# Attention scores of two steps side by side in PSUM, worked on in pairs

## The reference

```
xn  = layernorm(x)
q,k,v = xn @ Wq.T, xn @ Wk.T, xn @ Wv.T          16 heads of 32
s   = softmax(causal(q k^T / sqrt(32))) v         then @ Wo.T
h   = silu(xn @ W1.T) * (xn @ W3.T)               2048 wide
g   = silu(fwht(h) @ W2.T)                        Walsh-Hadamard transform of h
out = x + s * g
```

## Time and profile before

| | |
|---|---|
| runs (3) | median 944.87 us, 943.33 to 947.14 |
| profiled execution | 944.66 us, span 943.0 us |
| granted TensorE clock | 0.999 of full speed |
| busy share of the span | PE 98%, PEld 60%, DVE 77%, ACT 66%, POOL 36% |
| DMA | 110.09 MB, 117 GB/s in the mean |
| `heads` of batch one, of batch two | first score matmul at 88.4 us, at 556.3 us |

### The profile page before, as it was taken

How to read it: one execution, slowest core, us unless ns; L and a number is a source line. 1 busy time by engine, 2 the same in 40 slices (tenths; PEclk the granted TensorE clock), 3 DMA queues, 4 the chain that set the end, 5 groups by cost and what they waited for, 6 DMA issues and landing times. The chain is left out here.

```text
span 943.0 us, 19017 instructions
## 1 busy us (share of the span) xinstructions
PE 928.3 (98%) x6500; PEld 566.6 (60%) x6500; DVE 728.0 (77%) x1416; ACT 625.5 (66%) x1340; POOL 339.0 (36%) x591
## 2 busy tenths in 40 slices
PE   8999999999999999999999999999999999999997
PEld 7764566666666656744468656566665666575443
DVE  7886998998998988846665579989898899833343
ACT  4456889989889877833344358787887888833221
POOL 1896664665665442000000114344344353410000
PEclk9999999999999999999999999999999999999999
DMA  9797245544343414661236622323323232150111
GB/s 291 270 252 228 80 114 151 143 118 118 86 121 90 118 31 124 221 226 44 67 103 244 201 57 80 91 58 95 76 75 92 61 81 58 46 202 22 45 45 45
DMA packets 57920, 110.09 MB, mean 117 GB/s; under 512 B 5600, under 2 KB 22624, under 8 KB 57312
## 3 DMA queue, kind: packets, MB, share of 16 engines
q1 hardware_dynamic: 57824, 108.88, 38.9%
HBM read 79.23 MB, written 29.36 MB: 115 GB/s over the span
## 5 line engine op out<-in xcount | busy, mean ns | idle before, releaser
L1264 DVE TENSOR_TENSOR p_lo<-stages,p_hi 128x512 f16<-128x512 f32 (+2 forms) x288 | 201.7, 710 | 25.3 <-ACT p_hi L878 23.7
L1613 PE MATMUL f<-x_hi,w_lo 128*128 128x512 f16 x512 | 195.6, 382 | 0.0
L1613 PE MATMUL f<-x_lo,w_hi 128*128 128x512 f16 x512 | 194.8, 380 | 0.0
L1613 PE MATMUL f<-x_hi,w_hi 128*128 128x512 f16 x512 | 194.5, 380 | 0.0
L868 ACT ACTIVATE stages<-s 128x512 f32<-128x512 f32 (+2 forms) x288 | 150.6, 524 | 57.9 <-PE s L1573 55.5
L878 ACT ACTIVATE p_hi<-stages 128x512 f16<-128x512 f32 (+2 forms) x288 | 160.5, 557 | 25.6 <-POOL stages L699 16.4
L1573 PE MATMUL s<-qk_st 98*128 98x512 f32 (+2 forms) x384 | 129.9, 416 | 1.7 <-DMA qk_st<-m_lo 1.5
L699 POOL TENSOR_SCALAR_AFFINE_SELECT stages<-stages 128x128 f32<-128x128 f32 x192 | 61.4, 325 | 167.9 <-ACT stages L868 167.4
L707 POOL TENSOR_TENSOR w_lo<-w,w_hi 128x256 f16<-128x256 f32 x128 | 95.5, 775 | 55.2 <-ACT w_hi L931 52.8
L1251 DVE CUSTOM_DVE_ANT_0 m<-m,causal 128x1024 f32<-128x1024 f32 (+1 forms) x98 | 104.5, 1066 | 3.8 <-PE m L1554 2.7
L986 ACT ACTIVATE h_hi<-hidden 128x1024 f16<-128x1024 f32 x32 | 33.8, 1057 | 97.1 <-PE f L1411 97.1
(11 more groups left out here) (224 smaller groups left out, 1907.9 us busy)
## 6 DMA issues: line engine op xcount, KB each, us to landing
qk_st<-qk_parts SPq DMA_DIRECT2D x96, 256.0 KB, 4.3
w<-w1w SPq DMA_DIRECT2D x32, 512.0 KB, 3.6
qk_parts<-qk_hi SPq DMA_DIRECT2D x32, 256.0 KB, 3.5
qk_parts<-qk_lo SPq DMA_DIRECT2D x32, 256.0 KB, 4.4
scan<-w1w SPq DMA_DIRECT2D x12, 512.0 KB, 5.6
wht_in<-w SPq DMA_DIRECT2D x4, 1024.0 KB, 10.6
w_butterflied<-wht_in SPq DMA_DIRECT2D x4, 1024.0 KB, 5.7
x_in<-x SPq DMA_DIRECT2D x16, 256.0 KB, 2.9
```

Of the source, the lines that this page charges most:

```text
L1264: dve.tensor_tensor(p_lo[s][:], expd[q % NE][:, 0:end - need], p_hi[s][:], ALU.subtract).then_inc(p_lo_done, 1)
L1613: mm = pe.matmul(F[m][:, 0, :], w, v, start=k == 0, stop=k == GMM - 1)
```

## The change

Two steps, 2u and 2u + 1, make a pair u (6 in a head, NP). Their scores are written to two adjacent PSUM banks, the odd step's right-aligned in the first and the even step's left-aligned in the second, so that what is kept of both lies in one run of columns: 896, 384, 1024, 1024, 896 and 384 columns for pairs 0 to 5. PE issues the odd step's matmul first and signals once for the pair, and waits for the exponential of the whole pair before. One `exp`, one `probs_hi` and one `probs_lo` work on a pair: `exp` in ACT's slot 2u, `probs_hi` in ACT's slot 2u + 1, `probs_lo` in DVE's slot 2u + 1. One select masks both diagonal tiles of a pair. `expd` becomes two buffers of 1024 columns in room of their own, in place of four of 512 of which three were the `stages`. On SP the loads of w2 for the tail no longer wait for the last `probs_lo`. POOL's w13_low pieces wait for the exponentials of pairs 1 and 2, two pieces each, where they waited for those of steps 3, 4, 5 and 6. The two slab parts on POOL at a head's end come after the last mask and no longer between masks. Other counts in waits are rewritten from steps to pairs, the one of `transpose_ctx` (L1659) too, which is not shown.

```diff
...
 NS = len(STEPS)
+NP = NS // 2
 MAX_ORDER = [7, 0, 5, 1, 6, 2, 4, 3]
-NE = 4
+NE = 2
...
                 xt_lo = sb("xt_lo", [P, KT, S], F32R, q)
-            p_hi = [sb(f"p_hi{s}", [P, widths[s]], F16, r) for s in range(NS)]
-            p_lo = [sb(f"p_lo{s}", [P, widths[s]], F16, r) for s in range(NS)]
+            p_hi = [sb(f"p_hi{u}", [P, widths[2 * u] + widths[2 * u + 1]], F16, r) for u in range(NP)]
+            p_lo = [sb(f"p_lo{u}", [P, widths[2 * u] + widths[2 * u + 1]], F16, r) for u in range(NP)]
             squares = sb("squares", [P, 2 * D], F16, r)
-            sb("room_after_p", [P, 4 * KT * S - 2 * sum(widths) - 2 * D], F16, r)
+            expd = [sb(f"expd{i}", [P, 2 * W], F32, r) for i in range(NE)]
+            sb("room_after_p", [P, 4 * KT * S - 2 * sum(widths) - 2 * D - 4 * NE * W], F16, r)
...
             w13_lo = [w13_lo0, sb("w13_lo1", [P, 2, D], F16, r)]
-            expd = [*stage, sb("expd3", [P, W], F32, r)]
             scan = sb("scan", [P, 2, D], F32, r)
-            sb("room_before_o", [P, 5 * P], F32, r)
+            sb("room_before_o", [P, W + 5 * P], F32, r)
...
         F = [bank("f0"), bank("f1")]
-        SB = [bank("s0"), bank("s1")]
+        S_PAIR = bank("s", 2)
+        SB = [S_PAIR[:, i:i + 1, :] for i in range(2)]
...
-        def masks_before(n, s):
-            return n * NT + sum(diagonal(i) is not None for i in range(s))
+        def masked_pair(u):
+            return diagonal(2 * u) is not None
+        def masks_upto(n, u):
+            return n * (NT // 2) + sum(masked_pair(i) for i in range(u + 1))
+        def pair_widths(u):
+            return widths[2 * u + 1], widths[2 * u]
+        def in_pair(parts, s):
+            w1, w0 = pair_widths(s // 2)
+            return parts[s // 2][:, 0:w1] if s % 2 else parts[s // 2][:, w1:w1 + w0]
+        def pair_bank(u):
+            w1, w0 = pair_widths(u)
+            return S_PAIR[:].rearrange("p b w -> p (b w)")[:, W - w1:W + w0]
         def hidden_part(n, c):
...
                     if j + 2 < NH:
-                        after(sp, scores_ps, n * NS)
+                        after(sp, scores_ps, n * NP)
...
                                  ).then_inc(wo_in, 16)
-                sp.wait_ge(p_lo_done, (n0 + NH) * NS)
...
                     sp.wait_ge(wht_stored, D // P * 16)
+                    sp.wait_ge(w13_sum, SCAN_FIRST)
...
-            def mask(q):
-                pool.wait_ge(exp_done, q + 1)
+            def mask(n, u):
+                pool.wait_ge(exp_done, n * NP + u + 1)
                 pool.sem_inc(mask_begun, 1)
-                e = expd[q % NE][:, 0:P]
-                pool.affine_select(out=e, in_=e, compare_op=ALU.is_ge, fill=0.0, base=0, pattern=[[1, P]],
+                e = expd[(n * NP + u) % NE][:, 0:2 * pair_widths(u)[0]].rearrange("p (a c) -> p a c", a=2)[:, :, 0:P]
+                pool.affine_select(out=e, in_=e, compare_op=ALU.is_ge, fill=0.0, base=0, pattern=[[0, 2], [1, P]],
...
             def w13_low(n, piece):
...
             def heads(b):
...
                     n = b * NH + j
-                    for s in range(TPC):
-                        mask(n * NS + s)
+                    for u in range(TPC // 2):
+                        mask(n, u)
...
                         for piece in range(4):
-                            pool.wait_ge(exp_done, n * NS + 4 + piece)
+                            pool.wait_ge(exp_done, n * NP + 2 + piece // 2)
...
                         late_steps(1)
-                    mask(n * NS + 2 * TPC)
+                    mask(n, TPC)
                     combine(n, 0)
-                    for s in range(2 * TPC + 1, NS):
-                        mask(n * NS + s)
-                        if n < LAST_SLAB_AT - 1 and s >= NS - 2:
+                    mask(n, TPC + 1)
+                    for part in range(2):
+                        if n < LAST_SLAB_AT - 1:
...
                         of = j - LAST_SLAB_AT
-                        if b == 0 and 0 <= of < 8 and s >= NS - 2:
-                            slab_step(D // P - 1, of // 2, of % 2, s - NS + 2)
+                        if b == 0 and 0 <= of < 8:
+                            slab_step(D // P - 1, of // 2, of % 2, part)
...
             def exp(q):
-                c, k = STEPS[q % NS]
-                start, need, end = score_cols(c, k)
+                u = q % NP
...
                 after(act, p_lo_done, q - NE + 1)
-                act.activation(expd[q % NE][:, 0:end - need], SB[q % 2][:, 0, need - start:end - start],
-                               ACT.Exp).then_inc(exp_done, 1)
+                act.activation(expd[q % NE][:, 0:sum(pair_widths(u))], pair_bank(u), ACT.Exp).then_inc(exp_done, 1)
             def probs_hi(q):
-                n, s = divmod(q, NS)
-                _, need, end = score_cols(*STEPS[s])
+                n, u = divmod(q, NP)
                 act.wait_ge(exp_done, q + 1)
-                if diagonal(s) is not None:
-                    act.wait_ge(mask_done, masks_before(n, s) + 1)
-                after(act, pv_done, q - NS + 1)
-                act.activation(p_hi[s][:], expd[q % NE][:, 0:end - need], ACT.Copy
+                if masked_pair(u):
+                    act.wait_ge(mask_done, masks_upto(n, u))
+                after(act, pv_done, (n - 1) * NS + 2 * u + 2)
+                act.activation(p_hi[u][:], expd[q % NE][:, 0:sum(pair_widths(u))], ACT.Copy
...
             def copy_o(n, c):
...
                         copy_o(n0 + j - 1, 1)
-                    if g < SLOTS:
-                        exp(n0 * NS + g)
-                    if 1 <= g <= SLOTS:
-                        probs_hi(n0 * NS + g - 1)
+                    if g < SLOTS and g % 2 == 0:
+                        exp(n0 * NP + g // 2)
+                    if g < SLOTS and g % 2 == 1:
+                        probs_hi(n0 * NP + g // 2)
...
             def probs_lo(q):
-                s = q % NS
-                _, need, end = score_cols(*STEPS[s])
+                u = q % NP
                 dve.wait_ge(p_hi_done, q + 1)
-                dve.tensor_tensor(p_lo[s][:], expd[q % NE][:, 0:end - need], p_hi[s][:], ALU.subtract
+                dve.tensor_tensor(p_lo[u][:], expd[q % NE][:, 0:sum(pair_widths(u))], p_hi[u][:], ALU.subtract
...
             def split_wo(b, kt):
                 if kt == 0:
-                    dve.wait_ge(scores_ps, (b * NH + NH - 1) * NS)
+                    dve.wait_ge(scores_ps, (b * NH + NH - 1) * NP)
...
                         maxima(n0 + jm, r)
-                    if 1 <= g <= SLOTS:
-                        probs_lo(n0 * NS + g - 1)
+                    if g < SLOTS and g % 2 == 1:
+                        probs_lo(n0 * NP + g // 2)
...
             def scores(q):
-                n, s = divmod(q, NS)
-                c, k = STEPS[s]
-                start, _, end = score_cols(c, k)
-                if s == 0:
+                n, u = divmod(q, NP)
+                if u == 0:
                     pe.wait_ge(m_in, (n + 1) * 32)
-                after(pe, exp_done, q - 1)
-                pe.matmul(SB[q % 2][:, 0, 0:end - start], k_st[n % NH % 3][0:STACK + 2, k * P:(k + 1) * P],
-                          q_st[n % NH % 3][0:STACK + 2, start:end], start=True, stop=True).then_inc(scores_ps, 1)
+                after(pe, exp_done, q)
+                for s in (2 * u + 1, 2 * u):
+                    c, k = STEPS[s]
+                    start, _, end = score_cols(c, k)
+                    bank = SB[0][:, 0, W - (end - start):W] if s % 2 else SB[1][:, 0, 0:end - start]
+                    mm = pe.matmul(bank, k_st[n % NH % 3][0:STACK + 2, k * P:(k + 1) * P],
+                                   q_st[n % NH % 3][0:STACK + 2, start:end], start=True, stop=True)
+                mm.then_inc(scores_ps, 1)
             def context(q):
...
                     after(pe, o_copied, n * NC + c)
-                pe.wait_ge(p_lo_done, q + 1)
+                pe.wait_ge(p_lo_done, q // 2 + 1)
...
-                    pe.matmul(O[:, 0, first:first + VN], p_hi[s][:, at:at + P], v, start=k == 0 and t == c * TPC, stop=False,
+                    pe.matmul(O[:, 0, first:first + VN], in_pair(p_hi, s)[:, at:at + P], v, start=k == 0 and t == c * TPC, stop=False,
                               skip_group_check=True)
-                    mm = pe.matmul(O[:, 0, first + DH:first + VN], p_lo[s][:, at:at + P], v[:, DH:VN], start=False,
+                    mm = pe.matmul(O[:, 0, first + DH:first + VN], in_pair(p_lo, s)[:, at:at + P], v[:, DH:VN], start=False,
...
                 for g in range(SLOTS + DRAIN):
-                    if g < SLOTS - 2 and g % 2 == 0:
-                        scores(n0 * NS + g)
-                        scores(n0 * NS + g + 1)
-                    elif SLOTS - 2 <= g < SLOTS:
-                        scores(n0 * NS + g)
+                    if g < SLOTS and g % 2 == 0:
+                        scores(n0 * NP + g // 2)
```

(2 more changed lines are left out.)

## The result

The changed kernel takes 956.11 us (median of 4 runs, 954.81 to 958.44) against 944.10 for the kernel before, run beside it (943.07 to 947.14): a ratio of 1.0125, 95% interval [1.0093, 1.0156]. It is slower. The profiled execution, the fastest of the four, took 954.81 us, span 952.9, granted clock 1.00, against 944.66 and 943.0 before. The forecast was 950 between 940 and 966, so the sign and the range held, and the size came out 6 short.

The account below looks back on a forecast made before the run. TensorE, busy for 98% of the span, was taken to bound the kernel, so only its waits could be won. Stalls of 10.6 less gains of 5.1 on the profiled 944.66 us gave 950.2, said as 950, range 940 to 966.

Parts of the forecast that it names:

- place one: Pair 2's subtraction ahead of reduction 7: the maxima's transpose stalls 0.35 a head in batch two (5.3), 0.15 in one (2.3).
- Place two: Pair 4's subtraction ahead of reduction 0: next to nothing in the head read, less room in batch one; 0.1 x 30 = 3.
- What is gained: Waits of TensorE that go, at m_lo's DMA, in the last heads and in the tail: together 5.1 us, bounds 0 and 7.
- DMA waits for m_lo: m_lo reaches its DMA 0.7 us sooner, so these waits go: 1.8 us in batch two, 0.6 in batch one.
- passage to `tail`: First three w2 loads no longer wait for the last p_lo, so TensorE's 0.9 us wait for w_lo goes.
- last heads: Each batch's last head, without maxima between scores: about 0.4 lost to an exponential and 0.5 to the last p_lo; 1.8 for both.
- Off the path: Pairing saves 60 us of ScalarE and 25 of VectorE beside TensorE's columns, costed at nothing.
- The late request: Rival: pair 2's subtraction asks after 702.91, GpSimd's third w_lo piece goes first, 0.63 more a head; 969 us, chance 0.17.
- No effect: Rival: no new stall, and the DMA waits stay or are halved; 943 to 946 us, chance 0.12.
- no stall: Rival: pair 2's subtraction asks early or the margin holds, so only the 5.1 gain is left; 939.6 us, chance 0.26.
- The Trainium skill's rule: Rule cited against the change: where unsaturated engines cause bubbles on others, breaking up instructions may let work finish sooner; no size.

Follow-up runs that it names:

- lo_pair2_late: Changed kernel with only pair 2's p_lo subtraction one slot later, behind reduction 7; pair 4's stays ahead of reduction 0: 949.20 us, 1.0051 to the kernel before.
- lo_pair4_late: Changed kernel with only pair 4's p_lo subtraction one slot later, behind reduction 0; pair 2's stays ahead of reduction 7: 952.74 us, 1.0087 to the kernel before.
- lo_two_late: Changed kernel with the p_lo subtractions of pairs 2 and 4 one slot later, behind reductions 7 and 0: 944.89 us, 1.0009 to the kernel before.
- lo_two_ahead: Changed kernel with each pair's p_lo subtraction cut into its two steps, both kept in slot 2u + 1 ahead of the reduction: 977.14 us, one run.
- lo_behind_m: As lo_two_late, with pair 3's p_lo subtraction also later, in slot 8 behind m_lo: 969.13 us, 1.0269 to the kernel before.
- w_lo_memset: Changed kernel with GpSimd's four w_lo subtractions a head replaced by memsets writing zeros: 950.46 us, one run.

## Why the prediction was right, and where its sizes were off

**The mechanism, place one: right.** The forecast was that the pair's subtraction asks at 8.94 us into the head, gets in ahead of the third w_lo piece and holds reduction 7 back, for a stall of 0.35. Measured: it asks at 9.08, gets in ahead (GpSimd's third piece is the one that waits, 1.65 us long), and the transpose is 0.45 late. Select 0.40 predicted, 0.41 measured; exponential of pair 2 at 6.92, measured 6.93. In batch one 0.15 was predicted, 11.17 to 11.31 measured. Heads of batch two: 17.4 predicted, 17.48. The runs price place one at 6.9 us (changed against lo_pair2_late) or 7.8 (lo_pair4_late against lo_two_late); the prediction had 5.3 + 2.3 = 7.6.

**Place two: the term that was mis-sized.** The step was "0.1 x 30 = 3". In batch two it is right to the digit once nothing hides it (17.13 against 17.03), and next to nothing in the changed kernel, where the transposes' stall covers it: two delays of one engine were added that don't add. That batch two's sum still came out near is luck in part: its stall was 0.1 a head longer than forecast and its place two 0.1 shorter. In batch one it is too small, because I read the room from a quiet head of batch two and gave batch one the same sum. Batch one's 15 heads grew by 5.26; my terms for it made 2.3 + 1.5 - 0.6 = 3.2. The missing 2 lie in heads 1, 3 and 5 (18.35, 18.47, 18.46, before 17.57, 17.43, 17.41). Head 1, from the timelines of its engines:

```profile
118.38 2.26 POOL L705 TENSOR_TENSOR wht_in<-wht_in 128x512 f32<-128x512 f32 x1
...
120.59 0.40 POOL L719 TENSOR_SCALAR_AFFINE_SELECT expd<-expd 128x256 f32<-128x256 f32 x1
...
121.08 0.95 ACT L895 ACTIVATE p_hi<-expd 128x896 f16<-128x896 f32 x1 [1.17 <-issue]
...
122.06 1.09 DVE L1280 TENSOR_TENSOR p_lo<-expd,p_hi 128x896 f16<-128x896 f32 x1 [1.71 <-ACT p_hi L895]
123.07 1.23 DVE L1268 CUSTOM_DVE_ANT_0 m<-m,causal 128x1024 f32<-128x1024 f32 x1
...
124.41 0.61 PE L1570 MATMUL m<-qk_st 96*128 96x384 f32 x2 [0.53 <-DVE mx L1268]
```

Extra work of batch one on GpSimd (the slab part) stands ahead of the select, and every link behind it hands the delay on, now that the reduction comes last. In heads 3 and 5 the extra work is ACT's sum of squares, 1.04 us, ahead of the exponential of pair 3. lo_pair4_late, where the reduction no longer stands behind the chain, has 17.58 or 17.59 in all three heads: that the chain runs through place two is shown, though 1.2 of the 2.5 us that these three lose come back in heads 4 and 6. That the two pieces of extra work start it is read from the traces and not shown. The other 12 heads grew by 2.4, 0.20 each, where my terms make 3.2 / 15 = 0.21: the term was right for a quiet head of batch one and lacked its three busy ones.

**What is gained.** The DMA waits for m_lo went as forecast. So did the passage to `tail`: from the first output-projection matmul to the transform's first matmul 4.27 became 3.21, 1.06 less where 0.9 was forecast. The step that failed is the last heads: 1.8 less was forecast for both, 0.47 and 0.56 more came (from the last head's first scores to the first output-projection matmul: 15.94 to 16.41, 15.93 to 16.49). The last head of batch two:

```profile
828.40 1.01 ACT L887 ACTIVATE expd<-s 128x1024 f32<-128x1024 f32 x1
829.45 1.06 ACT L895 ACTIVATE p_hi<-expd 128x1024 f16<-128x1024 f32 x1
...
829.47 0.73 PE L1591 MATMUL s<-qk_st 98*128 98x512 f32 x2 [0.76 <-ACT expd L887]
...
833.64 0.50 PE L1591 MATMUL s<-qk_st 98*128 98x256 f32 x2 [0.28 <-ACT expd L887]
```

No maxima space the scores there, and a pair's scores need both PSUM banks, which come free together at the end of an exponential of 1.0 us. Before, the first bank came free after 0.6. The waits add up to it: TensorE loses 1.0 to exponentials in each last head, where only weight loads waited for them before, and no longer the 0.5 to the last p_lo, so 0.5 more a head. I had looked for what the old waits would lose, not for what a longer hold of the banks adds; the error is 2.8 us.

**The ledger.** Forecast +5.5 on the profiled execution, measured +10.15 (+9.9 in the span). The difference: last heads 2.8, batch one's heads 2.1, ahead of the first head 0.4, and the other way batch two's heads 0.5 (4.49 against 5.3 + 1.5 - 1.8 = 5.0) and the passage to `tail` 0.2. The medians lie 12.0 apart; the 1.9 beyond the profiled executions' difference are in no trace.

**Off the path.** ACT saved 21.7 us of busy time, not 60. The 0.31 that I gave to each removed pair of instructions counts both fixed costs, but records in a row overlap by 0.1 each, and 0.31 - 0.2 = 0.11 a pair, times 192, is 21. DVE saved 31.5, not 25, though the overlap takes 0.1 off each of 192 there too (the subtractions' records alone shrink from 249.4 to 200.5); the rest I read as less waiting at the port, since two subtractions of 512 columns took 0.85 each on average and one of 1024 takes 1.44. Neither touches the time.

**The rivals.** The late request (969) did not come: the request came 0.14 later than worked out, of 0.37 that would have tipped it, but GpSimd's second piece ended 0.09 later as well, at 9.40, as the prediction's argument against this rival had it. The margin was 0.32 in nearly every head. lo_two_ahead, where a second turn does go to GpSimd, shows what a lost turn costs together with a second fixed cost, 977. No effect and no stall fell with the rows of L1579. The Trainium skill's rule, page "Perfetto Trace Analysis", section "Optimizing Scalar/DVE Operations", that breaking up instructions may help where such an engine causes bubbles, holds only half here: broken up in the old slots the kernel gains 2.5 us of 12, with overlapping intervals, broken up in the same place it loses 21 more, in one run. What helps is moving the whole instruction.

## What to carry to other kernels

When instructions of an in-order engine are merged, the merged one stands at one place of its queue: list what used to run between the halves and what is now behind both, and check each consumer's slack against the added columns, in the busiest stretch and not in a quiet one. Choose the slot of the merged instruction anew; here that decision was worth 11 us and the merge itself nothing. A saving of busy time on engines with slack was worth nothing here, and merged buffers are held for as long as the merged instruction runs.

## What the runs showed of the hardware that I had not expected

- A GpSimd select of 0.41 us takes 1.68 when a two-input subtraction of DVE begins at about the same time (lo_behind_m; DVE's record starts at 708.63, the select's at 708.43), and the mean select in the changed kernel is 0.51. The wait at the port hits both sides: with 128 subtractions of GpSimd in each, their mean went from 0.775 us before to 0.886 in the changed kernel.
- GpSimd's memset of the same tile takes 0.31 us against a mean of 0.89 for the subtraction and 0.67 for one undisturbed, and DVE's subtractions of 1024 columns come down to 1.234 us on average (w_lo_memset).
- Two subtractions of 512 columns in a row took 1.95 us where one of 1024 took 1.39 (lo_two_ahead and the changed kernel, same place of a head): an instruction's end is where GpSimd's waiting one gets its turn, so fewer and longer instructions also mean fewer turns lost.
- A stall of DVE cost TensorE its clock: in lo_behind_m's last heads TensorE stood still for 2.4 and 1.9 us, and 1.2 and 0.4 us after it went on the granted clock fell from 1.00 to 0.50 (from 2.4 to 1.2 GHz) for 3.4 us; a 512-column matmul of the feed-forward took 0.63 us there in place of 0.38.
